# Edge scores copied out of the gather ring by GpSimd itself, ahead of the reuse of a place

## What is computed

```python
feat_all   = einsum('ni,rhid->rnhd', x, conv_weights)     # a row per node and edge type
feat_src_e = feat_all[edge_type, edge_src]                # one row per edge
el = sum(feat_src_e * attn_l[edge_type], -1)              # 4 source scores per edge
er = sum(feat_all[edge_type, edge_dst] * attn_r[edge_type], -1)
e  = leaky_relu(el + er, 0.2)
ex = exp(e - segment_max(e, edge_dst)[edge_dst])
alpha = ex / segment_sum(ex, edge_dst)[edge_dst]
h  = segment_sum(alpha[..., None] * feat_src_e, edge_dst) + h_bias
```

## Time and profile before

| | before |
|---|---|
| median of 3 runs | 2039.0 us (2038.72 to 2039.45) |
| profiled execution | 2046.73 us |
| its span, first to last instruction | 2045.0 us |
| TensorE / VectorE / ScalarE / GpSimd busy | 72% / 56% / 38% / 26% of the span |
| mean granted TensorE clock | 0.738 |

### The profile page before, as it was taken

One profiled execution on the slowest core, in us unless ns is written; L12 is line 12 of the kernel. 1 busy time (PEld: TensorE's weight loads), 2 busy tenths in 40 slices (PEclk: granted clock), 3 DMA queues, 4 the chain that ended last, 5 costly groups with the idle time before them and its releaser, 6 DMA issues.

```text
span 2045.0 us, 22094 instructions
## 1 busy us (share of the span) xinstructions
PE 1467.7 (72%) x5398; PEld 742.5 (36%) x5398; DVE 1154.6 (56%) x2998; ACT 779.0 (38%) x1163; POOL 523.6 (26%) x517
## 2 busy tenths in 40 slices
PE   6895888755545555555239999798998789889640
PEld 3443544110001010010128777554444344544430
DVE  5404443777767677776599988752261350530636
ACT  1332433655545555555110000035773337156021
POOL 0005344556646656666400000000000000000022
PEclk9995555655555555555559999898999989999875
DMA  3534333445544444544509888200000100000022
GB/s 143 170 141 139 128 113 121 148 145 165 163 133 148 154 143 154 171 152 154 170 28 314 273 273 268 78 1 22 1 1 1 31 0 1 1 1 1 11 57 61
DMA packets 74860, 223.92 MB, mean 109 GB/s; under 512 B 17384, under 2 KB 26516, under 8 KB 74260
## 3 DMA queue, kind: packets, MB, share of 16 engines
q1 hardware_dynamic: 50804, 158.00, 21.7%
q0 software_dynamic: 23968, 64.77, 11.8%
HBM read 140.09 MB, written 82.63 MB: 109 GB/s over the span
## 4 chain that ended last, share of the span: by engine, by line
PE 39%; DVE 13%; issue 6%; DVEq 2%; ACT 1%; POOL 1%; DMA 0%; another core or an unknown queue 0%; SPq 0%; POOLq 0%
PE bank L1673 14%; PE bank L1612 11%; PE bank L1693 2%; PE bank L1745 2%; PE bank L1657 2%; DVE arena L1079 1%; DVE arena L1037 1%; PE bank L1742 1%; DVE adjacency L1044 1%; DVE arena L1038 1%; PE bank L1731 1%; PE bank L1641 1%; POOL arena L523 1%; PE bank L1756 1%; ACT arena L605 1%
## 5 line engine op out<-in xcount | busy, mean ns | idle before, releaser
L523 POOL DMA_INDIRECT arena<-feat_table,arena x469 | 486.8, 1038 | 456.7 <-issue 240.4
L1554 PE MATMUL bank<-arena 128*128 128x480 f16 x586 | 336.6, 575 | 270.8 <-DVE arena L1038 161.1
L605 ACT ACTIVATE arena<-bank 128x480 uint16<-128x480 f32 x586 | 332.6, 572 | 274.9 <-PE bank L1554 172.6
L1044 DVE TENSOR_TENSOR adjacency<-adjacency,arena 128x480 uint16 x586 | 235.7, 402 | 131.8 <-issue 90.8
L1673 PE MATMUL bank<-arena 128*128 128x472 f16 x1440 | 294.9, 369 | 12.0 <-DVE arena L1228 8.1
L531 POOL DMA_INDIRECT arena<-al_table,edge_ends x15 | 14.5, 965 | 977.9 <-DMA al_table<-arena 973.7
L1554 PEld LDWEIGHTS bank<-arena 128*128 128x128 f16 x586 | 60.8, 104 | 546.8 <-DVE arena L1038 283.7
L1612 PE MATMUL bank<-arena 128*128 x966 | 229.3, 393 | 0.8 <-issue 0.3
L1673 PEld LDWEIGHTS bank<-arena 128*128 128x128 bf16 x1440 | 142.7, 99 | 164.4 <-issue 18.4
L1038 DVE TENSOR_SCALAR arena<-iota,arena 128x480 f16<-128x480 f16 x586 | 201.4, 344 | 0.0
L1612 PEld LDWEIGHTS bank<-arena 128*128 128x128 f32 x966 | 175.3, 191 | 55.1 <-issue 33.2
(11 more groups left out here) (291 smaller groups left out, 1533.6 us busy)
## 6 DMA issues: line engine op xcount, KB each, us to landing
edge_rows<-arena SPq DMA_DIRECT2D x67, 910.0 KB
arena<-edge_rows SPq DMA_DIRECT2D x117, 520.0 KB, 4.6
feat_table<-arena SPq DMA_DIRECT2D x60, 260.0 KB, 2.1
arena<-feat_table,arena POOLq DMA_INDIRECT x469
arena<-in_w SPq DMA_DIRECT2D x1, 2048.0 KB, 9.7
arena<-in_xT SPq DMA_DIRECT2D x1, 1920.0 KB, 18.2
arena<-in_x SPq DMA_DIRECT2D x1, 1792.0 KB
xt_table<-arena SPq DMA_DIRECT2D x3, 528.0 KB, 3.2
```

What stands on the lines that cost most here:

```text
L523: g.indirect_dma_start(out=SLOT[k][:, j, :], out_offset=None, in_=feat_t, in_offset=bass.IndirectOffsetOnAxis(ap=IE[:, GB * b + j:GB * b + ...
L605: a.activation(EV[st % AS].rearrange("p r k -> p (r k)"), PS[4 + st % 4][:, 0:R2 * KW], ACT.Copy)\
L1044: v.tensor_tensor(dst, dst, EV[st % AS], ALU.add).then_inc(s["a_add"], 1)
L1554: mm(PS[4 + st % 4][:, 0:R2 * KW], OHS[st % AS], OHK[st % AS], start=True, stop=True).then_inc(s["a_mm"], 1)
```

## The change

ScalarE's `collect` and the table of places where it stands go. GpSimd gets a `collect` of its own: at batch b, behind the wait for the store of the old batch, it copies the scores of batch b - 3 out of the place, waits for its own copy, and issues the seven gathers. The last three batches are copied behind the loop. SP waits once for `sc_mm` (the step transposes' products) ahead of its first read of rows, since ScalarE's copies no longer imply that.

```diff
-GC_ER, GC_ET, GC_LOOP = 10, 2, 62
...
                 if b == 0:
                     sp.wait_ge(s["collected"], NGB)
+                    sp.wait_ge(s["sc_mm"], SC)
...
+            def collect(b):
+
+                pool.wait_ge(g_done[b % NSLOT], BATCH * (b // NSLOT + 1))
+                g.tensor_copy(SUM[:, GB * b:GB * (b + 1), :], SLOT[b % NSLOT][:, :, D:FW]).then_inc(s["collected"], 1)
+
             for b in range(NGB):
                 k = b % NSLOT
                 if b >= NSLOT:
                     pool.wait_ge(r_st[k], 16 * (b // NSLOT))
+                    collect(b - NSLOT)
                     pool.wait_ge(s["collected"], b - NSLOT + 1)
...
+            for b in range(NGB - NSLOT, NGB):
+                collect(b)
...
-            def collect(b):
-
-                act.wait_ge(g_done[b % NSLOT], BATCH * (b // NSLOT + 1))
-                a.activation(SUM[:, GB * b:GB * (b + 1), :], SLOT[b % NSLOT][:, :, D:FW], ACT.Copy).then_inc(s["collected"], 1)
...
-                if g % 3 == 0 and g:
-                    collect(g // 3 - 1)
...
-                if c % 2:
-                    collect(GC_ER + c // 2)
...
-                    due = GC_ER + GC_ET + (GC_LOOP - GC_ER - GC_ET) * (AU * n + u + 1) // (A_N * AU)
-                    while got < due:
-                        collect(got)
-                        got += 1
...
-            for b in range(got, B_EARLY):
-                collect(b)
             for g in range(GR):
-                if g == G_EARLY:
-                    for b in range(max(got, B_EARLY), NGB):
-                        collect(b)
```

More of the change, by code:

```diff
@@ L609, in _ @@
                 a_evac(0, st)
-            got = GC_ER + GC_ET
             for n in range(A_N):
```

## The result

| | before | after |
|---|---|---|
| median | 2039.2 us (2038.7 to 2048.1) | 2435.2 us (2430.1 to 2441.6) |
| profiled execution, its span | 2046.7, 2045.0 | 2433.5, 2431.8 |
| ratio | | 1.193 [1.189, 1.198] |

What follows compares the result with a forecast made beforehand. Gathers end last, 17.20 us after the walk's chain, and GpSimd's waits end slow stretches. Walk's end 151 us later, less 17, is +134 on 2039.0: 2173; own range 2074 to 2318, 8-in-10 range 1997 to 2325.

Steps and rivals of the forecast that it cites:

- rival B: Table search starves, pace near 0.14 until gathers are through; walk ends at 1368, kernel about 2410; chance 0.08 including between-cases.
- What bounds the kernel, and the pause as cure: Gathers end last, 17.20 us behind the adjacency walk; GpSimd's 216.2 us of waits for ScalarE end slow stretches.
- GpSimd's copy: 67 score copies added to GpSimd's gather chain, 0.15 to 1.0 us each, taken as 0.4, together 27 us.
- rival C: GpSimd's copies hold up VectorE's adds in the walk: +13 us on rival A, 2021, or +23, 2031; chance 0.05.
- The burst's end: GpSimd's gathers run in one burst, 67 batches of 9.9 us, 663 us, ending near 821 instead of 1002.
- Rival D: GpSimd's copies take 3 us or more, its chain ends at 995: 2039, within a few us; chance 0.05.
- The end of the stage: Fourth lane product follows the third, giving back VectorE's idle 17.2 us if the walk's end stays.
- The work without disturbance: Search 157 us, the stage between 24 and the walk 458, together 639 us when nothing disturbs them.
- r: Pace of search and walk during the gather burst, 1 being full; taken as 0.5, range 0.28 to 0.65.
- The case for A: Sign that slow stretches don't grow: a four-place burst did 11 walk steps where others did 3 to 7.
- The case against B: Sign against a starved search at pace 0.14: the walk never fell as low.
- rival A: Slow stretches don't grow without GpSimd's pauses: r 0.75, walk ends at 966, 14 and 17 us won, 2008; chance 0.25.

Runs made afterwards that it cites:

- e1_third: Changed kernel, GpSimd held before each ring turn where the kernel before (2041.1 us in this job) made its copies: 2002.9 us, 0.981 of it.
- after_here: The changed kernel run again as it is, in a job where the kernel before took 1891.8 us: 1866.4 us, ratio 0.987.
- e2_again: Changed kernel with the first gather held until the search's last product, where the kernel before took 1891.8 us: 2006.3 us.
- e2_third: Changed kernel with the first gather held until the search's last product, where the kernel before took 2041.1 us: 2366.1 us.

## Why the prediction was wrong

The forecast was 2173; the measured 2435.2 is above the range's upper end of 2325. The direction was right, and rival B, with a chance of 0.08 and 2410, is what happened.

- *What bounds the kernel, and the pause as cure.* Right. The prediction read from the earlier trace rows that GpSimd's wait for ScalarE is what ends the slow stretches. `e1_third` shows it: with the waits back and the copies left in place the loss is gone.
- *GpSimd's copy.* Taken at 0.4 us, bounds 0.15 to 1.0; it is 0.217. 67 x 0.217 = 14.5 us, not 27. But none of these copies met the walk, which began behind the burst, so the official run says nothing on rival C. `after_here` does: 46 copies lie in its walk and take 0.505 us each, up to 0.72, and all 67 take 28.6 us. The adds beside a copy take 0.412 us, the others 0.408. GpSimd gives way and VectorE loses nothing to speak of; rival C is out, and 0.4 was a fair guess for a copy beside a full walk.
- *The burst's end.* 812 for 821, and 10.0 us a batch beside a full walk for 9.9. Rival D is out.
- *The end of the stage.* The 17.2 us are given back: from the last add to the end of the span it is 2431.8 - 1386.0 = 1045.8 against 2045.0 - 979.7 = 1065.3, that is 19.5.
- *The work without disturbance.* 639 taken; by after's own windows 32 groups x 4.0 = 128, 23 between, 462 for the walk, 613. The search's 4.9 us a group came from a stretch that was itself not free.
- *r, the step that failed.* By after's own terms 812 + 613 - 1386 = 39 us of work were done in the 649 us since 163, r = 0.06 instead of 0.5. Two things were wrong with the choice. First, r was taken from a row of the walk, "as the row nearest to what will run", though the burst begins in the search and ends all of itself there: a stage that falls hardly moves until the burst is over, so the stage met first sets r, and its row gave 0.14. With 0.14 the prediction's own sum gave 2410. Second, that row of 0.52 is not of an unbroken burst. In it GpSimd stood still for 1.71 us, and the walk came back for 5 us; the row is a mean of fall, recovery and fall. A timeline row and windows of L1038 of the kernel before, which take the row 547.00:563.50 apart:

```profile
554.80 0.94 POOL L523 DMA_INDIRECT arena<-feat_table,arena  x1 [1.71 <-issue]
...
549.00:554.80 5.80, 1.02 (x3) 0.50 0.46 131
554.80:560.00 5.20, 2.09 (x6) 0.50 0.75 256
560.00:563.50 3.50, 0.07 (x1) 0.50 0.41 112
```

For a burst of 655 us the pace inside the fall was the number to take: (3 + 7) steps in 25.3 us, 0.40 per us or 0.31 of 1.28, was in the earlier trace rows, and the walk's unbroken fall came out at 0.16.
- *The case for A* was read from the same row: "so the pace does come back with GpSimd still busy". It came back with GpSimd standing still, at 553.1 to 554.8.
- *The case against B* was that "the walk never fell as low". True of the rows, but the walk wasn't reached before the burst had ended.
- *What no row could tell.* r also depends on the supply that the job meets: under full supply it is 1 (`after_here`, and `e2_again` for the walk), the change gains 1.3%, and rival A's outcome holds (the gathers' chain ends last there, by 38 us, and comes earlier). The trace of the kernel before shows one condition only, and 1866 lies below the range as 2435 lies above it.

The Trainium skill, "Runtime: NRT & Kernel Launch", section Instruction fetch mechanics, holds that the sequencers fetch ahead by themselves and that the cost of this is mostly hidden. This case's trace doesn't contradict it, and speaks against a fetch that the gathers hold up. The profile lists the transfers of kind "instruction" by queue. From 200 to 800 us of after, in the fall, there are two of 16 KB on q8, of 1.26 and 0.96 us, where those outside take 0.88 to 1.65. From 400 to 940 of `e2_third`, in the fall of the walk, there is none on q8, and six on q14, as many as from 400 to 790 of `e2_again`, where nothing fell. The lines of the first two (packets, MB, share):

```profile
q8 instruction: 2, 0.03, 0.0%
...
q14 instruction: 6, 0.05, 0.0%
```

What is slow is each single instruction. VectorE's register operations at the add's line (DVEq is its sequencer; ns min/median/max), first of `e2_third` from 450 to 900 us, then of `e2_again` in the same stretch:

```profile
L1035 DVEq FUSED_REGOPS  x100: 3/701/1425, 449.6 to 898.5; - x100
L1035 DVEq FUSED_REGOPS  x426: 46/75/107, 450.3 to 793.6; - x142
```

It is the 0.70 us of the search again, in code that runs as a loop. So VectorE in the fallen walk and TensorE in the fallen search get on by about one instruction per 0.70 us. What takes the 0.70 us, and why it comes with one supply and not the other, no run shows.

## What to carry to other kernels

Before you free an engine that issues indirect gathers from a wait, look if the others regain their pace in its pauses: count steps of a neighbour in windows inside and behind its bursts. If they do, the wait is a brake that somebody needs; replace it by one that follows the neighbour's progress, closely, rather than drop it. And when a slow stretch inside a burst is carried to a longer burst, make sure that the engine never stands still in the row that you take, take the pace inside the fall and not a mean over it, and take it for the stage that the burst meets first.

## What was not expected

- The same kernel before took 1892 us in four jobs and 2039 to 2045 in the official one and two others, 8%, with the same instructions; its walk runs from 329 to 808 in the one and from 369 to 979 in the other. A change can be 0.987 on one side and 1.193 on the other.
- A fall is a state of its own: 1.27 steps per us, then 0.33, with gathers beside it in both. In the fall of the walk the gathers start every 1.25 us (0.95 + 0.30), at full pace every 1.47 (two steps of the walk). The quicker row alone does not make a fall: in `after_here`, under full supply, they start every 1.25 us all through the search, which keeps its full pace. Whether it holds up a fall that has begun was not tried.
- The search fell deeper (36 of some 476 matmuls in 100 us, 0.08) than the walk (20 of 127 steps, 0.16). VectorE and TensorE run the walk as a loop and the search unrolled, but the beat of 0.70 us gives both numbers without that. From 450 to 900 us of `e2_third` VectorE has 99 steps and some 6.7 instructions of all kinds to a step, 4.7 us by the beat, where a step takes 4.5 there. In the search of after the matmuls come 2.8 us apart, four beats. That is an estimate from counted records, and no run tried it.
- A plain transfer of the same 128 rows took GpSimd 0.54 us beside the search, against 0.95 to 1.1 for an indirect one, and all 469 were through by 517 us.
